# A fused attention and FP4 feed-forward kernel on one core: another order of the last steps, one rounding step less

## The reference

```python
x_proj = silu(x @ W1 + b1); u, v, q, k = split(x_proj, 4)
attn = silu(q k^T) / S                   # 16 heads of 8, no softmax
y = layernorm(av * u, gamma, beta) @ W2 + b2
x = layernorm(x + y)
h = silu(fp4(x) @ fp4(w_gate).T) * (fp4(x) @ fp4(w_up).T)      # 352 wide
x = layernorm(x + fp4(h) @ fp4(w_down).T)
```

## Time and profile before

| | |
|---|---|
| median of 3 runs | 527.5 us (527.36 to 527.96) |
| profiled execution | 526.95 us, span 524.9 us |
| ScalarE busy | 491.4 us, 94% of the span |
| TensorE busy | 502.4 us, 96% |
| VectorE busy | 210.9 us, 40% |
| GpSimd busy | 63.2 us, 12% |
| granted clock of TensorE | 1.00 |

### The profile page before, as it was taken

How to read it: one execution, slowest core, us unless ns; L and a number is a source line. 1 busy time by engine, 2 the same in 40 slices (tenths; PEclk the granted TensorE clock), 3 DMA queues, 4 the chain that set the end, 5 groups by cost and what they waited for, 6 DMA issues and landing times.

```text
span 524.9 us, 20049 instructions
## 1 busy us (share of the span) xinstructions
PE 502.4 (96%) x9056; PEld 265.2 (51%) x9056; DVE 210.9 (40%) x621; ACT 491.4 (94%) x558; POOL 63.2 (12%) x152
## 2 busy tenths in 40 slices
PE   7799999999999999999999999999999999999996
PEld 4453344444443444444443444444477777777753
DVE  4655552243433332243433332333343354544344
ACT  3899999999999999999999999999999999999920
POOL 6950000001010100101010100101010110101010
PEclk9999999999999999999999999999999999999999
DMA  4881240000000000000000000000000000000000
GB/s 125 229 186 33 62 121 2 1 3 6 2 7 2 7 2 8 1 2 7 2 8 1 7 1 7 1 3 8 1 9 4 9 9 3 10 2 9 4 7 6
DMA packets 13583, 12.12 MB, mean 23 GB/s; under 512 B 1589, under 2 KB 12858, under 8 KB 13498
## 3 DMA queue, kind: packets, MB, share of 16 engines
q1 hardware_dynamic: 12650, 9.05, 6.8%
...
q10 hardware_dynamic: 144, 0.13, 0.1%
HBM read 1.92 MB, written 1.05 MB: 6 GB/s over the span
## 4 chain that ended last, share of the span: by engine, by line
ACT 49%; PE 33%; issue 12%; DVE 3%; DMA 1%; POOL 1%; SPq 0%; POOLq 0%; DVEq 0%; ACTq 0%
ACT attn L611 48%; PE ps L382 31%; PE ps L396 2%; PE ps L430 1%; DMA k_stack<-parts 1%; POOL rstd_b L370 1%; DMA xn_b<-in_L_attn_b 0%; ACT feat L611 0%; DVE stats_b L780 0%; DVE parts L717 0%; POOL ve_b L369 0%; DVE mv_b L782 0%; DVE x_b L785 0%; ACT v_sb L611 0%; DVE magic_b L860 0%
## 5 line engine op out<-in xcount | busy, mean ns | idle before, releaser
L611 ACT ACTIVATE attn<-ps 128x1024 f32<-128x1024 f32 x512 | 478.4, 1195 | 3.5 <-PE ps L382 3.2
L382 PE MATMUL ps<-attn,v_pad 128*32 128x256 f32 (+1 forms) x5120 | 274.5, 341 | 0.4 <-DVE wdown_t L905 0.3
L382 PE MATMUL ps<-q_stack,k_stack 64*128 64x256 bf16 (+1 forms) x2560 | 173.7, 251 | 10.7 <-ACT attn L611 1.2
L382 PEld LDWEIGHTS ps<-attn,v_pad 128*32 128x32 f32 x5120 | 132.4, 109 | 80.2 <-issue 39.6
L382 PEld LDWEIGHTS ps<-q_stack,k_stack 64*128 64x128 bf16 x2560 | 78.4, 94 | 134.8 <-ACT attn L611 89.0
L369 POOL TENSOR_TENSOR ve_a<-mv_a,eps_col 128x1 f32<-128x1 f32 x24 | 4.5, 189 | 268.3 <-DVE mv_a L782 268.3
L830 DVE TENSOR_TENSOR gate_a<-gate_a,ps 128x352 f32<-128x352 f32 x8 | 4.2, 521 | 55.6 <-PE ps L382 55.6
L369 POOL TENSOR_TENSOR ve_b<-mv_b,eps_col 128x1 f32<-128x1 f32 x24 | 4.6, 190 | 175.6 <-DVE mv_b L782 175.6
L830 DVE TENSOR_TENSOR gate_b<-gate_b,ps 128x352 f32<-128x352 f32 x7 | 3.6, 521 | 47.0 <-PE ps L382 47.0
L382 PE MATMUL ps<-zeros 128*128 128x512 bf16 x63 | 15.7, 399 | 1.2 <-DVE zeros L851 1.2
L717 DVE CAST parts<-feat 128x512 bf16<-128x512 f32 (+1 forms) x10 | 6.8, 683 | 23.9 <-ACT feat L611 23.9
...
## 6 DMA issues: line engine op xcount, KB each, us to landing
...
```

The costliest lines, as they stand in the source:

```text
L382: return pe.matmul(to, lhsT, rhs, start=start, stop=stop, skip_group_check=True)
L611: return act.activation(to, frm, ACT.Silu, **kw)
```

## The change

1. A half step is now half of the m with both sets b (`group`), in scores and in the product with v; `times_v` waits for each half of attn by itself, and no longer for both at its start.
2. Down of tile 14 is taken out of the jobs and stands behind the last product with v. Its sum, statistics and last normalisation are written between the steps of tile 15 on VectorE, and `rstd` on GpSimd has the order to match.
3. `quantised_x` subtracts the mean, finds the largest values and scales them before it waits for 1/std, which then enters as a pointer operand. x1 is normalised behind it.
4. In `to_grid` the exponent is masked and set in one instruction with two bit operations; its lower bound is applied in the add and in the subtract, each now a scalar_tensor_tensor.
5. For tile 15, the turn of zu and y have banks and semaphores of their own; the three parts of hqT too, and the middle one is copied by VectorE.
6. Matmuls of zeros: none ahead of y (5 before), 22 ahead of the turn of x (27), 17 ahead of the turn of h (22), 1 ahead of down (2).

```diff
-    KEEP_WARM = {"y": 5, "xqT": 27, "gate": 2, "hqT": 22, "down": 2}
+    KEEP_WARM = {"xqT": 22, "gate": 2, "hqT": 17, "down": 1}
...
+    def group(c, g, a):
+
+        some = ms(c, g)
+        return [(m, b) for m in some[a * len(some) // 2:(a + 1) * len(some) // 2] for b in range(2)]
...
-    TILE_AT[DENSE] = (BEGIN[-2] + LAG, {"y": 0, "xqT": 4, "gate": 6, "up": 8, "hqT": 12, "down": 13})
+    TILE_AT[DENSE] = (BEGIN[-2] + LAG, {"y": 0, "xqT": 4, "gate": 6, "up": 8, "hqT": 12})
...
-            for tile in range(TAIL):
+            for tile in range(TAIL - 1):
                 for which in range(3):
                     rstd(ROWS[tile % 2], which)
-            for which in range(3):
-                rstd(ROWS[TAIL % 2], which)
+            before = ROWS[(TAIL - 1) % 2]
+            rstd(before, 0)
+            rstd(before, 1)
+            rstd(TAIL_ROWS, 0)
+            rstd(before, 2)
+            rstd(TAIL_ROWS, 1)
+            rstd(TAIL_ROWS, 2)
...
-                    for k, m in enumerate(ms(c, g)):
+                    for k, (m, b) in enumerate(group(c, g, a)):
                         for half in range(2):
                             rows = slice(64 * half, 64 * half + 64)
                             last = mm(ps[:, bank + half, k * w:(k + 1) * w],
-                                      k_stack[rows, M * a + m, i * P:(i + 1) * P],
-                                      q_stack[rows, M * a + m, Q0[c]:Q0[c] + w])
+                                      k_stack[rows, M * b + m, i * P:(i + 1) * P],
+                                      q_stack[rows, M * b + m, Q0[c]:Q0[c] + w])
...
                 w = WIDTHS[c]
-                pe.wait_ge(attn_ready, 2 * (at + 1))
                 if c == g == 0 and i % TPC == 0:
                     pe.wait_ge(v_padded, i // TPC + 1)
                 if g == i == 0:
                     wait_spare(AV[c], at + LAG)
-                for k, m in enumerate(ms(c, g)):
-                    for a in range(2):
+                for a in range(2):
+                    pe.wait_ge(attn_ready, 2 * at + a + 1)
+                    for k, (m, b) in enumerate(group(c, g, a)):
                         for half in range(2):
-                            cols = slice(32 * (2 * half + a), 32 * (2 * half + a) + 32)
+                            cols = slice(32 * (2 * half + b), 32 * (2 * half + b) + 32)
                             last = mm(ps[cols, AV[c], 0:w], v_pad[:, i, m, cols],
                                       attn[:, at % RING, a, half, k * w:(k + 1) * w],
...
-            keep_warm("y")
+            r = TAIL_ROWS
+            wait_job(job_no[("hqT", 0, TAIL - 1)])
+            down_of(ROWS[(TAIL - 1) % 2], BEFORE_TAIL_DOWN, 0).then_inc(before_tail_down, 1)
             pe.wait_ge(av_taken, len(WIDTHS))
-            for i in range(KT - TAIL):
-                y_of(TAIL + i, TAIL_SMALL[i], 0).then_inc(tail_y, 1)
+            z = zu[:, TAIL * P - Q0[-1]:KT * P - Q0[-1]]
+            turn_in_strips(TAIL_Z, 0, z).then_inc(tail_z, 1)
+            mm_rows(TAIL_Y, 0, z, w2_centred[:, :], P).then_inc(tail_y, 1)
             keep_warm("xqT")
...
+            pe.wait_ge(hq_ready, KT)
+            for t, (f0, fn) in enumerate(FT):
+                turn(TAIL_HQT[t], 0, r.xn[:, f0:f0 + fn], P, fn).then_inc(tail_hqT, 1)
             keep_warm("down")
-            for i, r in enumerate(TAIL_ROWS):
-                pe.wait_ge(tail_hqT_copied, i + 1)
-                down_of(r, TAIL_SMALL[i], 0).then_inc(tail_down, 1)
+            for t, (f0, fn) in enumerate(FT):
+                if t == 1:
+                    pe.wait_ge(tail_hqT_by_vec, 1)
+                else:
+                    pe.wait_ge(tail_hqT_by_act, t // 2 + 1)
+                last = mm_rows(TAIL_DOWN, 0, r.hqT[0:fn, t, :], wdown_t[0:fn, t, :], D, start=(t == 0), stop=(t == 2))
+            last.then_inc(tail_down, 1)
...
+            for t in (0, 2):
+                fn = FT[t][1]
+                act.wait_ge(tail_hqT, t + 1)
+                act.activation(r.hqT[0:fn, t, :], ps[0:fn, TAIL_HQT[t], 0:P], ACT.Copy).then_inc(tail_hqT_by_act, 1)
...
-                each(lambda t: dve.tensor_reduce(t.amax, t.src, AX_X, ALU.max, apply_absolute_value=True))
-                each(lambda t: dve.tensor_scalar(t.scale, t.amax, 1.0 / FP4_MAX, SCALE_MIN, ALU.mult, ALU.max))
-                each(lambda t: dve.reciprocal(t.rscale, t.scale))
-                each(lambda t: dve.scalar_tensor_tensor(out=t.xn_blocks, in0=t.src, scalar=JUST_BELOW,
-                                                        in1=t.wide_rscale, op0=ALU.mult, op1=ALU.mult))
-
-                each(lambda t: dve.tensor_scalar(t.magic.bitcast(U32), t.xn.bitcast(U32), EXPONENT, None,
-                                                 ALU.bitwise_and))
-                each(lambda t: dve.tensor_scalar(t.magic, t.magic, 1.0, 1.5 * 2.0 ** 22, ALU.max, ALU.mult))
-                each(lambda t: dve.tensor_tensor(t.xn, t.xn, t.magic, ALU.add))
-                each(lambda t: dve.tensor_tensor(t.xn, t.xn, t.magic, ALU.subtract))
...
+            def biggest(t):
+                return dve.tensor_reduce(t.amax, t.src, AX_X, ALU.max, apply_absolute_value=True)
+
+            def to_grid(t, factor, done):
+
+                link(dve.reciprocal(t.rscale, t.scale))
+                link(dve.scalar_tensor_tensor(out=t.xn_blocks, in0=t.src, scalar=factor, in1=t.wide_rscale,
+                                              op0=ALU.mult, op1=ALU.mult))
+                link(dve.tensor_scalar(t.magic.bitcast(U32), t.xn.bitcast(U32), EXPONENT, MAGIC,
+                                       ALU.bitwise_and, ALU.bitwise_or))
+                link(dve.scalar_tensor_tensor(out=t.xn, in0=t.magic, scalar=MAGIC_MIN, in1=t.xn,
+                                              op0=ALU.max, op1=ALU.add))
+                link(dve.scalar_tensor_tensor(out=t.xn, in0=t.magic, scalar=MAGIC_MIN, in1=t.xn,
+                                              op0=ALU.max, op1=ALU.subtract))
+                last = dve.scalar_tensor_tensor(out=t.dst, in0=t.xn_blocks, scalar=-1.0 / UP, in1=t.wide_scale,
+                                                op0=ALU.mult, op1=ALU.mult)
+                return last if done is None else last.then_inc(done, 1)
+
+            def fp4(t, done=None):
+                link(biggest(t))
+                link(dve.tensor_scalar(t.scale, t.amax, 1.0 / FP4_MAX, SCALE_MIN, ALU.mult, ALU.max))
+                return to_grid(t, JUST_BELOW * UP, done)
...
+            def quantised_x(r):
+
+                centred = r.gate[:, 0:D]
+                t = Blocks(centred.rearrange("p (b k) -> p b k", k=BLOCK),
+                           r.xn[:, 0:D].rearrange("p (b k) -> p b k", k=BLOCK), P, NBD, r)
+                wait_mean()
+                link(dve.tensor_scalar(centred, r.x1p[:, :], r.mv[:, 1, 0:1], JUST_BELOW * UP, ALU.subtract, ALU.mult))
+                link(biggest(t))
+                link(dve.tensor_scalar(t.amax, t.amax, 1.0 / (FP4_MAX * JUST_BELOW * UP), None, ALU.mult))
+                dve.wait_ge(rstd_ready, rstd_no.next())
+                link(dve.tensor_scalar(t.scale, t.amax, r.rstd[:, 1:2], SCALE_MIN, ALU.mult, ALU.max))
+                to_grid(t, r.rstd[:, 1:2], xq_ready)
+                link(normalise(r.x1p[:, :], r.x1[:, :], 1, r))
...
+            r, before = TAIL_ROWS, ROWS[(TAIL - 1) % 2]
+            dve.wait_ge(tail_z, 1)
+            statistics(ps[:, TAIL_Z, 0:P], 0, r)
+            dve.wait_ge(before_tail_down, 1)
+            link(dve.tensor_tensor(before.x1p[:, :], ps[:, BEFORE_TAIL_DOWN, 0:D], before.x1[:, :], ALU.add))
+            statistics(before.x1p[:, :], 2, before)
+            dve.wait_ge(tail_y, 1)
+            link(y_plus_x(r, ps[:, TAIL_Y, 0:P], TAIL))
+            statistics(r.x1p[:, :], 1, r)
+            rstd_before = rstd_no.next()
+            quantised_x(r)
+            dve.wait_ge(rstd_ready, rstd_before)
+            finish(TAIL - 1)
+            dve.wait_ge(tail_silu, 1)
+            dve.wait_ge(tail_up, 1)
+            link(dve.tensor_tensor(r.gate[:, :], r.gate[:, :], ps[:, TAIL_UP, 0:FF], ALU.mult))
+            quantised_h(r)
+            dve.wait_ge(tail_hqT, 2)
+            dve.tensor_copy(r.hqT[:, 1, :], ps[:, TAIL_HQT[1], 0:P]).then_inc(tail_hqT_by_vec, 1)
+            dve.wait_ge(tail_down, 1)
+            link(dve.tensor_tensor(r.x1p[:, :], ps[:, TAIL_DOWN, 0:D], r.x1[:, :], ALU.add))
+            statistics(r.x1p[:, :], 2, r)
+            dve.wait_ge(rstd_ready, rstd_no.next())
+            finish(TAIL)
```

110 lines of the change are left out of this document (33 added, 77 removed).

## The result

The changed kernel takes 523.92 us (median of 6 runs, 523.74 to 525.64), the kernel before 527.43 in the same comparison (6 runs, 527.27 to 528.26). The ratio is 0.9925 with a 95% interval of 0.9908 to 0.9941, which of 527.4 is 3.1 to 4.9 us less; the profiled execution took 523.74 us with a span of 521.7, where the one before took 526.95 with 524.9. The forecast was 2.9 us less, 524.6, with a range down to 523.9. The direction was right and the size too small: the ratio makes 523.5 of the 527.5 that the forecast started from, 0.4 under the range; with its interval that is 522.6 to 524.4, of which the upper part lies in the range. The gain has three sizes here: 3.2 between the two profiled executions, 3.5 between the medians, 4.0 by the ratio.

The account below looks back on a forecast made before the run. ScalarE was taken to bound the loop, a chain of single steps on tile 15 the tail. 1.27 + 0.13 + 0.84 - 0.2 + 0.38 + 0.48 = 2.90 us off 527.5 gives 524.6; range 523.9 to 525.5 (8 in 10).

Parts of the forecast that it names:

- the start of the tail: From the last attn to the turn of zu: down of tile 14 and zeros out of the way, gain 1.27 us.
- FP4 of h: In the tail, one VectorE operation less in the FP4 of h: gain 0.38 us.
- hqT and down: Tail, turn of h to the sum: copies by thirds make 2.12 into 1.63, gain 0.48 us.
- the clock: Rival in the tail: fewer zeros lower the granted clock, some 3 us of matmuls double, 527.5, no change; chance 0.03.
- The same in all other tiles is off the path: Loop: the shorter FP4 in tiles other than 15 gains nothing, as ScalarE sets the loop.
- FP4 of x: Tail, normalisation to turn of x: 2.99 becomes 2.15, gain 0.84 us, before 0.2 taken off for contention.
- The rival of a loop gain: Loop: TensorE waits for VectorE's shorter FP4, so the loop gains too, 523.0 to 524.0; chance 0.03.
- I take -0.2: Tail, 1/std beside FP4 of x: VectorE and GpSimd disturb each other at shared SBUF interfaces, loss 0.2 us, bounds 0 and 0.5.
- Statistics at 503.98: Tail: statistics of z wait only for the turn of zu, not for y, and start at 503.98; gain 0.13 us.
- cost 0: Tail: tile 14's add and statistics fit into VectorE's 0.93 us wait for 1/std, 0.05 left; GpSimd's swapped order also free.
- the port in full: Rival in the tail: both engines hold each other, 0.5 not 0.2, and tile 14's cover slips 0.1; 525.0, chance 0.2.
- the slower loop: Rival: the second wait for attn breaks the run of weight loads; 533.6 at 0.2 a wait, chance 0.04.

Follow-up runs that it names:

- half_only: The kernel before with only scores and products with v changed to half steps: 528.42 us, ratio 1.0004 to the kernel before.
- down14_job: The changed kernel with down of tile 14 a job again, its VectorE steps ahead of zu, 1/std in the old order, no zeros ahead of y: 525.44 us.
- no_half: The changed kernel with scores and products with v by whole steps again: 525.53 us, ratio 0.9946 to the kernel before.
- zeros_back: The changed kernel with five matmuls of zeros again between down of tile 14 and the turn of zu: 526.01 us, ratio 0.9962.
- single_waits: The changed kernel with one wait, not two, at x1p of tile 15 and at the scale of FP4 of x: 525.09 us, ratio 0.9930.
- stats14_late: The changed kernel with sum, statistics and last norm of tile 14 moved behind FP4 of tile 15's x: 525.07 us, ratio 0.9952.

## Why the prediction was right or wrong

Right: that the loop is ScalarE's, but for the places near 415 and 476 us, and the satisfied waits are free (half_only); the start of the tail, its place and its cause (down14_job, no_half, zeros_back); FP4 of h, 0.38 forecast and 0.38 seen; hqT and down, 0.48 forecast and 0.49 seen, with 1.63 from turn to sum as worked out; that the clock stays (the stretches are below). zu was worked out at 0.77 behind the last attn and came at 0.77. The sum was 2.90, the span fell by 3.2. Two readings in the prediction are off by little and change nothing: the 64 loads take 1.77, which is 0.01 over twice 0.88 and not under it, and the 2.63 adds up ten rows, the normalisation and nine steps.

Where it was off:
- **"The same in all other tiles is off the path"** is the step that failed as a mechanism. Near 415 us zu stands behind the FP4 of x and TensorE behind zu; the loop ended 0.2 earlier, 0.17 of it behind the mark. The rival of a loop gain had a chance of 0.03, since "the waits show nothing of the kind". The timeline did: 0.44 labelled issue at the load, and zu as the releaser at its matmul.
- **"I take -0.2"**, for the port. GpSimd was not held, 0.19 and 0.56 for its two steps. What was lost is 0.09 between bn_aggr and the scale (1.20 for 1.11), the price of a second wait on the scale step (single_waits), which the prediction did not have. FP4 of x with its wait gained 0.75 where 0.84 - 0.2 = 0.64 was forecast.
- **"Statistics at 503.98"**: from the last attn on the gain was 1.51 where 1.27 + 0.13 = 1.40 was forecast. The 96 loads ended at 502.45, 0.43 behind the last attn where 0.53 was worked out, so the turn of zu started 1.11 behind it and not 1.18; from there to the statistics it took 0.54 and not 0.58.
- **"cost 0"** for tile 14's steps was right (stats14_late), but x1p was 0.08 late by the second wait on it.
- **The range.** The first three and the 0.08 at x1p make 0.2 + 0.11 + 0.11 - 0.08 = 0.34, of the 0.35 between 2.90 and the 3.25 that the parts add up to (hqT has the last 0.01). The rest of the miss is not in the profiles: 0.3 up to the difference of the medians (3.51), 0.7 up to the 4.0 of the ratio. The start of the program varies by up to 2.2 us, with the granted clock in it, and the range, made of costs in the tail alone, left no room for that. The profiled runs of both kernels are of the early kind (mark at 49.0, no fall of the clock), so their 3.2 is free of it.

The rivals fell: the port in full by the add and pow in the changed kernel, which keep their lengths, the clock by the granted clock of 1.00 in the pauses and in the first 1.7 us behind the last matmul, the slower loop by half_only. Later the clock falls (0.68 from 519.30 to 521.20), with no matmul left to slow. The copies of hqT in thirds were not taken back in a run; their 0.49 is read from the timeline alone. TensorE by stretch in the changed kernel (length, busy us and count, granted clock, DMA share, GB/s):

```profile
503.75:517.50 13.75, 12.14 (x77) 1.00 0.02 7
517.60:519.30 1.70, 0.00 (x0) 1.00 0.00 0
```
